# A gated cross-attention block with a ternary feed-forward part: signals, order and engine of small steps in the query projection

## The reference

```
t    = layernorm(x)
q    = (t Wt + bt) * mask        k, v = split((ctx Ws + bs) * mask)      8 heads of 64
a    = softmax(q k / 8, masked keys at -inf) v
x    = x + tanh(g_xattn) * (concat(t, a) Wo + bo)
u    = layernorm(x)
h    = silu(conv3(int8(u) @ ternary(W1)) + conv_b)                       2048 channels
out  = x + tanh(g_ffn) * (int8(h) @ ternary(W2))
```

## Time and profile before

| | us |
|---|---|
| median of 3 runs | 1792.73 (1792.53 to 1796.08) |
| the profiled execution | 1785.82 |
| its span, from the first to the last instruction | 1784.0 |
| PE busy | 1646.3 |
| DVE, ACT, POOL busy | 1148.9, 818.8, 718.9 |

### The profile page before, as it was taken

The page is one execution under the profiler, slowest core; times in us unless marked ns, Lnnn a source line. Parts: engine busy times, 40 slices in busy tenths (PEclk is TensorE's granted clock), DMA queues, the critical chain, the costliest instruction groups (busy, mean ns, idle before and its releaser), DMA issues. The chain is left out here.

```text
span 1784.0 us, 23923 instructions
## 1 busy us (share of the span) xinstructions
PE 1646.3 (92%) x8713; PEld 1012.4 (57%) x8754; DVE 1148.9 (64%) x2199; ACT 818.8 (46%) x866; POOL 718.9 (40%) x314
## 2 busy tenths in 40 slices
PE   6999999999998999999999999999998686986867
PEld 5778788888885544454445444454455443544434
DVE  7788734444427677657866687567528749399792
ACT  3121213222210444424563455436647777787776
POOL 1221000000000688756875677657935326062250
PEclk9999999999999999999999999999999898998989
DMA  7777555444443322202232213212234020020201
GB/s 264 259 270 235 192 186 185 167 169 165 159 153 114 143 82 86 84 1 107 78 108 77 107 61 107 84 52 92 73 118 142 25 95 12 17 91 1 95 1 48
DMA packets 108583, 200.87 MB, mean 113 GB/s; under 512 B 8384, under 2 KB 33984, under 8 KB 108480
## 3 DMA queue, kind: packets, MB, share of 16 engines
q1 hardware_dynamic: 108480, 199.49, 32.0%
HBM read 124.75 MB, written 74.71 MB: 112 GB/s over the span
## 5 line engine op out<-in xcount | busy, mean ns | idle before, releaser
L745 POOL TENSOR_TENSOR acc<-acc,pr 128x1024 f32<-128x1024 f32 x188 | 448.7, 2387 | 134.2 <-ACT pr L777 117.5
L777 ACT ACTIVATE pr<-ps,mcol 128x1024 f32<-128x1024 f32 x256 | 284.2, 1114 | 366.4 <-PE ps L1507 363.6
L1044 DVE CUSTOM_DVE_ANT_0 junk<-ps,mbias 128x512 bf16<-128x512 f32 x512 | 333.0, 688 | 128.5 <-PE ps L1482 124.1
L1519 PE MATMUL ps<-pr,vv 128*64 128x512 f32 x1024 | 275.3, 619 | 0.0
L752 POOL TENSOR_TENSOR h_first<-h_first,last_tap 128x1023 f32<-128x1023 f32 x44 | 103.6, 2357 | 252.5 <-DVE h_first L1396 222.9
L726 POOL MEMSET nmt<- 128x128 f32 x1 | 0.2, 206 | 346.3 <-DVE chl L1281 346.3
L1482 PE MATMUL ps<-kh,qh 64*128 64x512 f32 x512 | 123.0, 451 | 13.1 <-DVE nmv L1044 12.0
L1589 PE MATMUL ps<-xiT,w1q 128*128 128x512 bf16 x491 | 117.6, 380 | 12.5 <-ACT xiT L767 5.7
L745 POOL TENSOR_TENSOR acc<-pr 128x1024 f32<-128x1024 f32 x32 | 76.8, 2400 | 121.4 <-ACT pr L777 121.4
L1482 PEld LDWEIGHTS ps<-kh,qh 64*128 64x128 f32 x512 | 50.9, 184 | 130.8 <-issue 99.3
L1753 PE MATMUL ps<-w2q,hq 128*128 128x512 bf16 x492 | 117.1, 388 | 3.5 <-ACT hq L955 2.3
(11 more groups left out here) (173 smaller groups left out, 3145.2 us busy)
## 6 DMA issues: line engine op xcount, KB each, us to landing
craw<-in_ctxT SPq DMA_DIRECT2D x8, 2048.0 KB, 8.8
xa<-in_x SPq DMA_DIRECT2D x32, 256.0 KB, 3.8
wraw<-in_w1T SPq DMA_DIRECT2D x16, 512.0 KB, 5.9
wraw<-in_w2T SPq DMA_DIRECT2D x16, 512.0 KB, 7.1
q_split<-kqh SPq DMA_DIRECT2D x32, 256.0 KB, 2.0
q_split<-kql SPq DMA_DIRECT2D x32, 256.0 KB, 2.3
base<-lna SPq DMA_DIRECT2D x32, 256.0 KB, 3.4
k_split<-kqh SPq DMA_DIRECT2D x32, 256.0 KB, 2.1
```

Of the source, the lines that this page charges most:

```text
L745: nc.gpsimd.tensor_tensor(acc[:, blk % 2, :], first, pr[:, (8 * blk + j) % NP, :], ALU.add).then_inc(pool_acc, 1)
L777: act.activation(pr[:, u % NP, :], ps[:, 2 * (u % 2):2 * (u % 2) + 2, :].rearrange("p a t -> p (a t)"), ACT.Exp, bias=mcol[:, (u // 64) * ...
L1044: dve.tensor_tensor_reduce(out=(junk1 if n < LEAD and n % 2 else junk)[:, e, :], in0=ps[:, first_bank(n) + e, :], in1=mbias[:, b % 2, kk * ...
L1519: last = pe.matmul(ps[64 * e:64 * e + 64, 6 + blk % 2, :], vv[g % 2][:, j, 64 * e:64 * e + 64], pr[:, u % NP, e * CH:(e + 1) * CH], start= ...
```

## The change

It does five things, all in the query stage.

- The identity matrix gets its own semaphore, `sp_ident`. PE waits for it alone before the first transposes, ACT before its copy of the identity. DVE waits for the other constants (112) where it scales the output bias.
- SP issues the two gate transfers behind the first two weight transfers, no longer ahead of x.
- ACT begins with a square root of a constant (`sqrt_table(0)`), which has the square root's table loaded, ahead of the root for chunk 0. Tanh of the gates comes in chunk 0, behind the four `weight_hi`, and is followed by another such square root and by the copy of the identity.
- The absolute sums go from DVE to ACT: an ACTIVATE with Abs in place on `wraw`, with its accumulator written to `wabs`. In the chunks 0 to 6 they stand behind `lth` number 1 and number 2, in the last chunk behind the four `kqh`. A semaphore of their own, `act_wabs`, replaces their steps in DVE's count, for SP's loads of `wraw` and for DVE's final sum in the next stage.
- In chunk 0 DVE does `norm` of chunk 1 ahead of scaling the output bias and of the four additions; in the other chunks the order stays.

```diff
--- before.py
+++ after.py
@@ -238,6 +238,8 @@
 
         sp_gates = sem("sp_gates")
         sp_const = sem("sp_const")
+        sp_ident = sem("sp_ident")
+        act_wabs = sem("act_wabs")
         act_const = sem("act_const")
         dve_const = sem("dve_const")
         sp_wstage = [sem(f"sp_wstage{i}") for i in range(2)]
@@ -334,7 +336,7 @@
         A_DVE = {}
         n = 0
         for name in ([f"xb{j}" for j in range(CT)] + ["q0", "q1", "ql0", "q2", "ql1", "q3", "ql2", "ql3"]
-                     + ["base0", "wabs1", "base1", "wabs2", "base2", "base3"]):
+                     + ["base0", "base1", "base2", "base3"]):
             n += 1
             A_DVE[name] = n
         A_DVE_N = n
@@ -474,13 +476,13 @@
                     sp.wait_ge(pool_split, 2 * (i - 1 - N_FAST))
                 sp.dma_start(stage(i, splits[i][0]), splits[i][0]).then_inc(sp_wstage[i % 2], 16)
 
+            for j in product_order(0):
+                load_x(0, 0, j)
+            sp.dma_start(ident[:], ident_d[:, 0:P]).then_inc(sp_ident, 16)
+            for i in range(2):
+                load_split(i)
             for i, g in enumerate((g_x, g_f)):
                 sp.dma_start(graw[:, i:i + 1], g.rearrange("(a n) -> a n", a=1).broadcast_to([P, 1])).then_inc(sp_gates, 16)
-            for j in product_order(0):
-                load_x(0, 0, j)
-            sp.dma_start(ident[:], ident_d[:, 0:P]).then_inc(sp_const, 16)
-            for i in range(2):
-                load_split(i)
             for dst, src in ((bo[:], b_out.rearrange("(a n) -> a n", a=1).broadcast_to([P, D])),
                              (bq[:], bq_cols),
                              (bk[:], bk_cols),
@@ -512,7 +514,7 @@
                 else:
                     sp.dma_start(maskb[:], mask[ds(b, 1), CH:S].broadcast_to([P, CH])).then_inc(sp_maska, 16)
                 if c:
-                    sp.wait_ge(dve_a, (c - 1) * A_DVE_N + A_DVE["wabs2"])
+                    sp.wait_ge(act_wabs, 2 * c)
                 for i, src in enumerate((w1_flat, w2_flat)):
                     sp.dma_start(wraw[:, i, :], src[ds(c * P, P), :]).then_inc(sp_wraw, 16)
 
@@ -613,7 +615,8 @@
 
             sp.wait_ge(pool_split, POOL_ALL)
             sp.dma_start(bv[:], b_v.rearrange("(a n) -> a n", a=1).broadcast_to([P, D])).then_inc(sp_bconst, 16)
-            sp.wait_ge(dve_a, (NCH - 1) * A_DVE_N + A_DVE["wabs2"])
+            sp.wait_ge(dve_a, (NCH - 1) * A_DVE_N + A_DVE[f"q{PAIRS - 1}"])
+            sp.wait_ge(act_wabs, 2 * NCH)
             load_maskb(0, 0)
             load_wraw(0)
             for j in range(CT):
@@ -839,7 +842,10 @@
                         act.activation(lth[:, k, 0:CH], ps[:, k, :], ACT.Copy).then_inc(act_th, 1)
                     for i in range(N_FAST // 2, N_FAST):
                         weight_hi(i)
-                    act.wait_ge(sp_const, 128)
+                    act.wait_ge(sp_gates, 32)
+                    act.activation(cst[:, 0:2], graw, ACT.Tanh).then_inc(act_const, 1)
+                    sqrt_table(1)
+                    act.wait_ge(sp_ident, 16)
                     act.activation(identb[:], ident[:], ACT.Copy).then_inc(act_const, 1)
                 if not last:
                     std(c + 1)
@@ -854,14 +860,26 @@
                             act.wait_ge(pe_ab, c * CT + CT + p)
                             act.wait_ge(dve_tl, c * CT + CT + p)
                         act.activation(lth[:, :, turned(1 - slot, j)], ps[:, 0:KD, j * P:(j + 1) * P], ACT.Copy).then_inc(act_th, 1)
+                        if p in (1, 2):
+                            weight_sum(c, p - 1)
+                else:
+                    for i in range(2):
+                        weight_sum(c, i)
+
+            def weight_sum(c, i):
+                if i == 0:
+                    act.wait_ge(sp_wraw, c * 32 + 32)
+                act.activation(wraw[:, i, :], wraw[:, i, :], ACT.Abs, accum_out=wabs[:, i, ds(c, 1)]).then_inc(act_wabs, 1)
+
+            def sqrt_table(i):
+                act.activation(cst[:, 13 + i:14 + i], eps, ACT.Sqrt, bias=eps)
 
             def weight_hi(i):
                 act.wait_ge(sp_wstage[i % 2], 16 * (i // 2 + 1))
                 act.activation(splits[i][1], stage(i, splits[i][1]), ACT.Copy).then_inc(act_wh, 1)
 
-            act.wait_ge(sp_gates, 32)
-            act.activation(cst[:, 0:2], graw, ACT.Tanh).then_inc(act_const, 1)
             act.wait_ge(dve_const, 1)
+            sqrt_table(0)
             std(0)
             for i in range(N_FAST // 2):
                 weight_hi(i)
@@ -1202,13 +1220,14 @@
                         dve.tensor_tensor(ltl[:, k, 0:CH], ps[:, k, :], lth[:, k, 0:CH].bitcast(F32), ALU.subtract).then_inc(dve_tl, 1)
                     for i in range(N_FAST // 2, N_FAST):
                         weight_lo(i)
+                    norm(b + slot, 1 - slot)
                     dve.wait_ge(act_const, 1)
-                    dve.wait_ge(sp_const, 128)
+                    dve.wait_ge(sp_const, 112)
                     dve.tensor_scalar(bo[:], bo[:], gate_x, None, ALU.mult).then_inc(dve_const, 1)
                     dve.wait_ge(dve_const, 2)
                 for j in order:
                     dve.tensor_tensor(xa[:, slot, j, :], xa[:, slot, j, :], bo[:], ALU.add).then_inc(dve_a, 1)
-                if not last:
+                if not (first or last):
                     norm(b + slot, 1 - slot)
 
                 def q(m):
@@ -1235,10 +1254,6 @@
                     dve.wait_ge(dve_a, dn + A_DVE[f"xb{p}"])
                     dve.scalar_tensor_tensor(out=lna[:, order[p], :], in0=ps[:, 4 + p, :], scalar=gate_x, in1=xa[:, slot, order[p], :],
                                              op0=ALU.mult, op1=ALU.add).then_inc(dve_a, 1)
-
-                def weight_sum(i):
-                    dve.tensor_reduce(wabs[:, i, ds(c, 1)], wraw[:, i, :], AX.X, ALU.add,
-                                      apply_absolute_value=True).then_inc(dve_a, 1)
 
                 dve.wait_ge(sp_maska, c * 16 + 16)
                 q(0)
@@ -1251,13 +1266,10 @@
                 q_low(3)
                 if not last:
                     dve.wait_ge(pe_at, c * KD + 2 * KD)
-                dve.wait_ge(sp_wraw, c * 32 + 32)
                 for p in range(CT):
                     if not last:
                         turned_low(p)
                     base(p)
-                    if p < 2:
-                        weight_sum(p)
 
             for j in range(CT):
                 dve.sem_inc(sp_base_out[j], 16)
@@ -1318,6 +1330,7 @@
             split_lo(0, 0)
 
             N = 1.0 / (D * HID)
+            dve.wait_ge(act_wabs, 2 * NCH)
             dve.tensor_reduce(wmean, wabs[:], AX.X, ALU.add).then_inc(dve_const, 1)
             dve.wait_ge(pe_wsum, 1)
             dve.tensor_scalar(wmean, ps[:, 7, 0:2], N, 1e-5, ALU.mult, ALU.max).then_inc(dve_const, 1)
@@ -1628,7 +1641,7 @@
 
             pe.sem_inc(pe_ab, CT)
             pe.sem_inc(pe_bv, 8)
-            pe.wait_ge(sp_const, 128)
+            pe.wait_ge(sp_ident, 16)
             turn(0)
             pe.wait_ge(dve_wl, 2)
             for slot in range(2):
```

## The result

The changed kernel takes 1779.98 us in the median of six runs (1778.46 to 1782.23), the kernel before 1792.63 in the six beside it (1789.21 to 1796.08). The ratio is 0.9925, with a 95% interval of 0.991 to 0.994: 12.7 us faster by the medians. The prediction had the direction, and 7.3 us.

A forecast was written before the change was run, and what follows sets the result against it. PE was taken as the bound, busy 92% of the span, with its loss in query-stage waits, mostly for `ltl`. Gains of 3.2 + 1.1 + 3.0 = 7.3 us took the median from 1792.73 to 1785.4, range 1782.0 to 1789.5.

The forecast's parts named there:

- The sum: Whole kernel: 3.2 + 1.1 + 3.0 = 7.3 us gained, profiled execution to 1778.5, median to 1785.4.
- the gain doesn't depend on which: Whole kernel: the same 7.3 us come off the profiled execution and the median, which is 6.9 above it.
- The clock: Chunk 1's query matmuls: the wait before them stays 3.3 us, so the clock fall behind it still costs 1.6.
- Sums on ScalarE: VectorE's chain from first to fourth `ltl`: absolute sums moved to ACT shorten it from 6.86 to 5.75, 1.1 per chunk.
- 3.2 at Q1: Query stage: chunk 1's query matmuls start at 42.4, 3.2 us earlier, through start, norm and shorter chain.
- T0 and the tables: Start: chunk 0's transposes come 2.76 us earlier, at 9.96; loading the square-root table before the data takes 1.30 off the path.
- B0: Query stage: chunk 0's base matmuls start at 27.9 instead of 31.13, 3.2 us earlier.
- the start is bound by DMA: Rival, start: weights queued behind x come 0.93 us earlier, not 2.2; gain 6.0, 1786.7; chance 0.15.
- Carried to the end: Later stages: they start when the query stage ends, so its 7.3 us gain arrives at the end undiminished.
- Abs in another table: Rival, sums on ACT: two table loads per sum, chain 3.8 us longer, some 23 slower, 1816; chance 0.03.
- the drain behind a switch: Rival, ACT in chunk 0: each table switch takes 2.66 us with a drain; gain 5.3, 1787.4; chance 0.05.
- The clock stays up: Rival, chunk 1's query matmuls: no clock fall, gain 7.3 + 1.6 = 8.9, up to 10.5; 1783.5; chance 0.22.

The follow-up runs named there:

- before_again: The kernel before, unedited, run and profiled again: 1791.6 us median, ratio 1.0001.
- start_alone: The kernel before with only the identity's own semaphore, the later gate transfers and the new table order: 1795.0 us, ratio 1.0010 to the kernel before.
- norm_alone: The kernel before with only the norm of chunk 1 moved ahead of the bias scaling and additions: 1792.6 us, ratio 0.9998.
- start_and_norm: The changed kernel with the absolute sums back on VectorE: 1794.2 us, ratio 1.0004 to the kernel before.
- before_forced: The kernel before with GpSimd's splits waiting for the chunk's first query block, to bring `wsl` over `kql`: 1794.5 us, ratio 1.0017.
- before_pool_late: The kernel before with GpSimd's splits of a chunk waiting for the chunk's last `kql`: 1783.5 us, ratio 0.9933 to the kernel before.
- after: The changed kernel itself, with all five parts of the change, against the kernel before: 1779.98 us, ratio 0.9925.
- after_pool_late: The changed kernel with GpSimd's splits of a chunk waiting for the chunk's last `kql`: 1771.8 us, ratio 0.9872 to the kernel before.

## Why the prediction was wrong

- **The sum.** The step that failed is "the gain doesn't depend on which" execution. I priced everything on one execution at 1785.8, one of the kernel's fastest. By the mean clock, an average run of the kernel before spends some 100 us at the lower level, the profiled one 88; the profiles of kernels that can't be told from it in time (`before_again`, `start_alone`, `norm_alone`, `start_and_norm`, `before_forced`) show one to four more waits of 2 us or above than the earlier trace rows. `before_pool_late` says what this is: one wait on GpSimd is worth 1.9 between the profiled executions and 11.7 in the medians. The changed kernel has lost most of it too, so it gains 5.6 against the profiled execution and 12.7 in the medians.
- **The other term left out** is the time of `kql` beside GpSimd, which I put at nothing but luck. With it the query stage of the profiled pair gains 2.4, not 7.3. That the pair gains as much as 5.6 is luck of another kind: 3.5 come from the wait in the attention that nobody foretold.
- **The clock.** From a fall behind 3.27 and none behind 2.55 I took it that the short waits are harmless and left only Q1 in doubt, for 1.6. In the profiles of this study waits between 1.8 and 2.8 us in front of Q were followed by the lower level in 12 of 17 cases, none up to 1.7 was. In the changed kernel itself Q2 fell after 1.89. A rule made from two rows was too much. The size was right behind these waits (Q takes 12.6 to 12.8 instead of 11.2), and too small behind the 5.21, where Q1 takes 13.6.
- **Sums on ScalarE.** Mechanism right: no table load, the chain shorter, Q4 to Q7 without waits, the last chunk covered, `chl` at 1.66 still. The saving in the chain is 6.86 - 5.14 = 1.7 instead of 1.1, since Abs took 1.05 and most of the accumulator's read lies beside the next instruction.
- **3.2 at Q1.** T0 and the tables were right. PE was even free 1.4 earlier than foretold in front of T1, but `lna` was not ready. B0 came 0.9 short, because the weights for the two `wo1h` came 1.0 and 1.3 earlier and not 2.2 (the rival "the start is bound by DMA" had this). The rest went in the `kql` that GpSimd stretched, and at Q1 0.4 was left. The stretch isn't to be seen in the earlier trace rows; it stood in the rows right behind, shown above, and these I had before me.
- **Carried to the end.** Not as I said it. Behind the query stage the fourteen profiles take 1561 to 1568, a spread as large as the whole forecast. In the main pair this part changed by 3.2, and in `after` and `after_pool_late` by nothing. So what the query stage gains arrives at the end, give or take a few us that the attention and the clock add.
- **Rivals.** The slower one, Abs in another table, is excluded: there is no table load at L872. So is the drain behind a switch. *The clock stays up* is wrong for Q1, whose clock fell. Its 1783.5 should be 1783.8 for a gain of 8.9, and the 10.7 of the range should be its 10.5.

The stretch is a behaviour of VectorE and GpSimd that the Trainium skill (SBUF — State Buffer, Who interferes with whom) describes: a VectorE instruction with two SBUF inputs contends with a GpSimd instruction that reads SBUF, one with at most one SBUF input, outside the modes that use two ports, does not. The traces agree. `kql`, two inputs from SBUF, takes 2.58 beside `wsl` and 0.69 alone. `ltl`, which reads PSUM and SBUF, keeps its 0.69 beside `wsl` in `after_pool_late`, and there the four additions `xa<-xa,bo`, again two inputs from SBUF, take 3.77 together instead of 2.50, where nobody waits for them.

## What to carry to other kernels

A gap of two microseconds on PE can be the visible end of a loop: a late engine costs the clock, and the slower PE moves the next chunk's work under someone else's. Ask of each transfer and each GpSimd instruction that is free to float where it lands when PE is 2 us late, and pin it with a wait where it can't hurt; here one wait was worth about as much as the whole change. And before a difference is priced on one profile, look at the spread of the runs and at the clock of each: a kernel that varies by 1% has several courses, and a profile shows one. Look, too, for the gain where you didn't expect it: more than half of this pair's lay in a stage that the change doesn't touch.

## What the runs showed of the hardware that I had not expected

- The clock fell to its lower level (matmuls of 512 columns 0.43 us apart, 1.2 GHz) behind waits as short as 1.89 us, and stayed up behind others of 2.5 to 2.6. In `norm_alone` it fell behind 2.08 and stayed up behind 2.52, so the wait's length alone doesn't decide.
- ACT_TABLE_LOAD takes 1.28 and the next ACTIVATE starts 0.02 later, also when two loads follow each other closely (18.64 to 21.46).
- Reading ScalarE's accumulator is an instruction of its own of 0.19 us, and starts 0.10 before its ACTIVATE ends; the pair occupies 1.14 us, and the next copy starts 0.10 before that is over.
- Of a VectorE and a GpSimd instruction that collide, the one that starts first keeps its time: `kql` 0.02 ahead of `wsl` took 0.69 and `wsl` 2.94; `kql` 0.39 behind it took 2.58 and `wsl` 2.41. An instruction of 128 x 8 values can cost 2.36 us in this way.
